# Routed-expert blocks: gathers for six more experts, weight halves on VectorE, evictions on ScalarE, and another order at the turn into the blocks

## What is computed

```python
scores = softmax(xt @ router_w + router_b) + router_bias      # 16 experts in 4 groups
# keep the 2 best groups, then the 2 best experts; vals = their scores; gate = vals scattered
def step(y, p):                                               # for each of the 16 experts
    h = silu(xt @ w1 + b1) * (xt @ w2 + b2)
    return y + ge[:, None] * (h @ w3 + b3)
z = (silu(xt @ sw1 + sb1) * (xt @ sw2 + sb2)) @ sw3 + sb3     # shared expert
```

## Time and profile before

| | |
|---|---|
| median of 3 runs | 608.7 us |
| profiled execution | 612.38 us, its span 610.6 us |
| mean granted TensorE clock | 0.992 |
| PE / DVE / ACT / POOL busy | 562.1 / 408.7 / 345.2 / 349.6 us |
| blocks, first matmul after the turn to last eviction | 110.6 to 184.6 us of the span |
| HBM read / written | 56.94 / 15.20 MB |

### The profile page before, as it was taken

How to read it: one execution, slowest core, us unless ns; L and a number is a source line. 1 busy time by engine, 2 the same in 40 slices (tenths; PEclk the granted TensorE clock), 3 DMA queues, 4 the chain that set the end, 5 groups by cost and what they waited for, 6 DMA issues and landing times.

```text
span 610.6 us, 11610 instructions
## 1 busy us (share of the span) xinstructions
PE 562.1 (92%) x3232; PEld 273.6 (45%) x3232; DVE 408.7 (67%) x1049; ACT 345.2 (57%) x858; POOL 349.6 (57%) x371
## 2 busy tenths in 40 slices
PE   2999998798969989999868999999999999999997
PEld 0445444576644444444313444444444344444453
DVE  6898756494535965555689999999999900001782
ACT  4575866543432276777666777877777723142131
POOL 5993375788956237989844544445444534477011
PEclk9999999899989999999989999999999999999999
DMA  9996289999968206989599999999999984342001
GB/s 338 413 383 244 53 214 199 253 383 408 396 236 308 89 10 181 204 202 214 114 224 175 180 169 182 180 178 183 180 179 182 174 172 167 105 152 87 2 1 69
DMA packets 211622, 118.78 MB, mean 195 GB/s; under 512 B 188017, under 2 KB 196337, under 8 KB 208642
## 3 DMA queue, kind: packets, MB, share of 16 engines
q1 hardware_dynamic: 209122, 108.58, 70.6%
q0 software_dynamic: 2288, 9.70, 4.3%
q10 hardware_dynamic: 176, 0.04, 0.0%
HBM read 56.94 MB, written 15.20 MB: 118 GB/s over the span
## 4 chain that ended last, share of the span: by engine, by line
PE 39%; POOL 19%; DVE 13%; issue 11%; SPq 8%; DMA 5%; ACT 4%; DVEq 0%; POOLq 0%; ACTq 0%
PE ps L358 12%; PE ps L360 11%; PE ps L359 11%; SPq L513 8%; POOL hlr L1317 5%; POOL wsp L1317 5%; POOL q_sb L1317 3%; PE ps L667 2%; PE ps L540 2%; POOL xs_dram L1358 1%; POOL pT L1317 1%; POOL q_sb L1334 1%; DMA stage<-in_moe,disp 1%; DMA wsp<-hlr 1%; POOL q_sb L1430 1%
## 5 line engine op out<-in xcount | busy, mean ns | idle before, releaser
L1188 ACT ACTIVATE f32r<-f32r,mneg 128x512 f32<-128x512 f32 x128 | 91.5, 715 | 29.0 <-DVE mneg L1895 29.0
L1317 POOL TENSOR_TENSOR wsp<-stage,wsp 128x512 f16<-128x512 f32 (+1 forms) x69 | 78.4, 1166 | 49.0 <-ACT wsp L1159 44.1
L1895 DVE CUSTOM_DVE_ANT_0 f32r<-ps,nmask 128x512 f32<-128x512 f32 x128 | 82.4, 680 | 1.5
L1453 POOL TENSOR_SCALAR hlr<-f32r,rinv 128x512 f16<-128x512 f32 x64 | 44.8, 708 | 48.9 <-DVE rinv L1900 45.1
L1453 POOL TENSOR_SCALAR stage<-f32r,rinv 128x512 f16<-128x512 f32 x64 | 43.6, 691 | 47.5 <-DVE rinv L1900 42.9
L1317 POOL TENSOR_TENSOR hlr<-f32r,hlr 128x512 f16<-128x512 f32 x36 | 41.3, 1158 | 44.5 <-ACT hlr L1269 33.6
L358 PE MATMUL ps<-q_sb 128*128 128x512 f16 x132 | 50.7, 384 | 14.6 <-POOL q_sb L1317 12.0
L358 PE MATMUL ps<-k_sb,q_sb 128*128 (+1 forms) x128 | 49.5, 387 | 11.7 <-DVE mneg L1895 8.9
L1905 DVE SCALAR_TENSOR_TENSOR hlr<-f32r,rinv,hlr 128x512 f16<-128x512 f32 x64 | 50.1, 818 | 1.3 <-POOL hlr L1453 1.3
L1905 DVE SCALAR_TENSOR_TENSOR stage<-f32r,rinv,stage 128x512 f16<-128x512 f32 x64 | 49.2, 807 | 2.3 <-POOL stage L1453 2.3
L360 PE MATMUL ps<-q_sb 128*128 128x512 f16 x132 | 50.5, 383 | 0.0
(11 more groups left out here) (365 smaller groups left out, 1427.1 us busy)
## 6 DMA issues: line engine op xcount, KB each, us to landing
stage<-in_wq SPq DMA_DIRECT2D x8, 1024.0 KB, 6.1
stage<-in_wo SPq DMA_DIRECT2D x8, 1024.0 KB, 4.8
q_sb<-in_moe SPq DMA_DIRECT2D x9, 768.0 KB, 9.1
xs_dram<-zeros SPq DMA_DIRECT2D x1, 5888.0 KB, 28.8
pT<-xs_dram SPq DMA_DIRECT2D x23, 256.0 KB, 7.5
r_dram<-f32r SPq DMA_DIRECT2D x23, 256.0 KB, 7.0
k_sb<-in_wkv SPq DMA_DIRECT2D x3, 1024.0 KB, 18.8
stage<-in_moe SPq DMA_DIRECT2D x4, 768.0 KB, 10.1
```

The lines of the kernel that those rows point to most:

```text
L1188: act.activation(f32r[:, j % 4, :], f32r[:, j % 4, :], ACT.Exp, bias=mneg[:, j % 4:j % 4 + 1], scale=-1.0, accum_out=psum_col[:, j % 4:j % ...
L1317: return pool.tensor_tensor(dst_lo, src, dst_hi, ALU.subtract)
L1453: pool.tensor_scalar(halves(j)[:, 0, :], f32r[:, j % 4, :], rinv[:, 0, j % 4:j % 4 + 1], PSCALE, ALU.mult, ALU.mult).then_inc(s_ph, 1)
L1895: dve.tensor_tensor_reduce(f32r[:, j % 4, :], ps[j % 4][:, :], nmask[:, qt, :], 0.125, BIG, ALU.add, ALU.min, mneg[:, j % 4:j % 4 + 1]).th ...
```

## The change

Weights of experts 8 to 12 and 14 are now gathered by POOL like those of the spill blocks. The row numbers that the gather uses lie beyond the table's end for an expert with no token, and for an unused spill block (the limit to expert 15 is gone); `bounds_check` with `oob_is_err=False` leaves such rows out. The lo halves from block 4 on are DVE's, the evictions ACT's; POOL keeps the lo halves of blocks 0 to 3, and those of 2 and 3 now stand in the key phase. At the turn ACT takes `silu(0)` ahead of the hi casts of key tiles 13 and 14, and DVE turns the rows of blocks 0 to 2 and gates block 0 ahead of normalising key tile 15.

```diff
+GATHERED = [8, 9, 10, 11, 12, 14] + list(range(E_ROUTED, NB))
 ...
@@ SP
-                if r == 13:
+                if r == 12:
                     load_slots(4)
 ...
-                    if BEFORE[m] == n - 2 and not E_ROUTED <= m < NB:
+                    if BEFORE[m] == n - 2 and m not in GATHERED:
                         load_expert(m)
@@ ACT
                         if ahead and r == r0 + tiles * iters - 1:
-                            ahead()
-                        if not first or j >= 1 + lag:
+                            ahead[0]()
+                            hi(r - 2, i, j - 2, first)
+                        if (not first or j >= 1 + lag) and not (ahead and r == r0 + tiles * iters - 2):
                             hi(r - 1 - lag, i if j >= 1 + lag else i - 1, (j - 1 - lag) % tiles, first)
 ...
+                if ahead:
+                    ahead[1]()
 ...
-                      {2: router_exponentials, 12: gates_split, 14: lambda: w12_hi(2)}, lambda: silu(0))
-            for n in range(1, NB):
+                      {2: router_exponentials, 12: gates_split, 14: lambda: w12_hi(2)},
+                      (lambda: silu(0), lambda: (w12_hi(3), silu(1))))
+            def evict(n):
+                act.wait_ge(s_dn, n + 1)
+                if n >= 3:
+                    act.wait_ge(s_rst[n % 3], 16 * (n // 3))
+                act.copy(f32r[:, n % 3, :], ps[n % 4][:, :]).then_inc(s_re, 1)
+            for n in range(2, NB):
                 silu(n)
                 w12_hi(n + 2)
+                evict(n - 2)
@@ POOL
+                if r == 14:
+                    w12_lo(2)
 ...
+                    if beside and j == 0:
+                        w12_lo(3)
 ...
+                i = GATHERED.index(n)
+                if i >= 4:
+                    pool.wait_ge(s_wi[i % 4], 16 * (i // 4))
+                rows = widx[:, n - E_ROUTED:n - E_ROUTED + 1] if n >= E_ROUTED else own_rows[:, n:n + 1]
+                pool.indirect_dma_start(landed_at(n, slice(0, EG)), None, moe, bass.IndirectOffsetOnAxis(ap=rows, axis=0),
+                                        bounds_check=E_ROUTED * P - 1, oob_is_err=False).then_inc(s_wi[i % 4], 16)
-            for n in range(NB):
-                w12_lo(n + 2)
-                for m in range(E_ROUTED, NB):
-                    if BEFORE[m] == n - 2:
-                        gather_expert(m)
+            for n in GATHERED:
+                gather_expert(n)
@@ DVE
+                link(dve.tensor_scalar(unowned, ps[6][:, NT * E_ROUTED:(NT + 1) * E_ROUTED], 0.0, 65536.0, ALU.is_equal, ALU.mult))
+                dve.scalar_tensor_tensor(out=own_rows, in0=first_slot, scalar=lane_less, in1=unowned, op0=ALU.add, op1=ALU.add)
 ...
-                link(dve.tensor_scalar(owner, owner, float(E_ROUTED - 1), None, ALU.min))
 ...
+            def first_rows():
+                slots_turned(0)
+                slots_turned(1)
+                gated(0)
+                slots_turned(2)
-                                            15: lambda: slots_turned(0)})
+                                            15: first_rows})
+            def w12_lo(n):
+                dve.wait_ge(s_w12h, n + 1)
+                for u in range(2):
+                    at = slice(u * KC * INTER, (u + 1) * KC * INTER)
+                    last = dve.tensor_tensor(split_at(n, 1, at), landed_at(n, at), split_at(n, 0, at), ALU.subtract)
+                last.then_inc(s_w12l, 1)
-            for n in range(NB):
-                if n + 1 < NB:
+            for n in range(1, NB):
+                if 2 < n + 1 < NB:
                     slots_turned(n + 1)
                 gated(n)
+                if n == 2:
+                    dve.wait_ge(s_w12l, 4)
+                if n >= 2:
+                    w12_lo(n + 2)
                 if n in (4, 6, 8):
                     (small_lows, owners_biases, pair_gates)[n // 2 - 2]()
-                if n >= 2:
-                    evict(n - 2)
```

More of the change, by code:

```diff
@@ L156, in xattn_ffn_kernel @@
         lane = disp[:, 56:57]
+        lane_less = disp[:, 57:58]
+        own_rows = sml[:, 0, :].bitcast(I32)
+        unowned = sml[:, 1, :]
         first_slot = disp[:, 60:60 + E_ROUTED]
@@ L378, in wait_landed @@
         def wait_landed(engine, n):
-            if E_ROUTED <= n < NB:
-                engine.wait_ge(s_wi[n % 4], 16 * ((n - E_ROUTED) // 4 + 1))
+            if n in GATHERED:
+                engine.wait_ge(s_wi[GATHERED.index(n) % 4], 16 * (GATHERED.index(n) // 4 + 1))
             else:
                 engine.wait_ge(s_we[LAND[n]], (32 if LAND[n] == 7 else 16) * (
-                    1 + sum(LAND[m] == LAND[n] and not E_ROUTED <= m < NB for m in range(n))))
+                    1 + sum(LAND[m] == LAND[n] and m not in GATHERED for m in range(n))))
         def wait_landing_free(engine, n):
@@ L1135, in _ @@
             rms_phase(0, 2, 8, 1.0 / HD, scs[:, 12:13], s_kT, True, True, None,
-                      {2: router_exponentials, 12: gates_split, 14: lambda: w12_hi(2)}, lambda: silu(0))
-            for n in range(1, NB):
+                      {2: router_exponentials, 12: gates_split, 14: lambda: w12_hi(2)},
[6 more added lines that the diff above has]
+            for n in range(2, NB):
                 silu(n)
                 w12_hi(n + 2)
+                evict(n - 2)
+            evict(NB - 2)
+            evict(NB - 1)
             def shared_silu(n, bank):
@@ L1546, in _ @@
             dve.tensor_copy(lane, ranked[:, E_ROUTED:E_ROUTED + 1])
+            dve.tensor_scalar(lane_less, ranked[:, E_ROUTED:E_ROUTED + 1], -1.0, None, ALU.add)
             dve.tensor_scalar(first_slot, ranked[:, 0:E_ROUTED], float(P), 1.0, ALU.mult, ALU.add)
@@ L1789, in slots_turned @@
                 dve.tensor_copy(words(turned(n)), ps[4 + n % 2][:, :].rearrange("p (l w) -> p l w", l=2)).then_inc(s_xTc, 1)
-            rms_phase(0, 2, 8, True, True, {3: scores_of_experts, 4: gates, 5: slot_numbers, 12: gates_turned, 13: owners,
-                                            15: lambda: slots_turned(0)})
-            def small_lows():
-                dve.wait_ge(s_mask, 16)
-                dve.tensor_scalar(nmask[:, :, :], nmask[:, :, :], -8.0, None, ALU.mult).then_inc(s_ol, 4)
-                dve.wait_ge(s_gh, 1)
-                dve.tensor_tensor(gatesT[1], gateT[0:E_ROUTED + 1, :], gatesT[0], ALU.subtract).then_inc(s_gl, 1)
             def bias(a, n):
@@ L1812, in gated, with small_lows @@
                                          in1=hidden[n % 3], op0=ALU.add, op1=ALU.mult).then_inc(s_hx, 1)
+            def first_rows():
[3 more added lines that the diff above has]
+                slots_turned(2)
+            rms_phase(0, 2, 8, True, True, {3: scores_of_experts, 4: gates, 5: slot_numbers, 12: gates_turned, 13: owners,
+                                            15: first_rows})
+            def small_lows():
+                dve.wait_ge(s_mask, 16)
+                dve.tensor_scalar(nmask[:, :, :], nmask[:, :, :], -8.0, None, ALU.mult).then_inc(s_ol, 4)
+                dve.wait_ge(s_gh, 1)
+                dve.tensor_tensor(gatesT[1], gateT[0:E_ROUTED + 1, :], gatesT[0], ALU.subtract).then_inc(s_gl, 1)
             def w3_lo(n):
```

10 lines of the change are left out of this document (removed).

## The result

The changed kernel took 607.28 us (median of 19 runs, 604.36 to 620.92), the kernel before, beside it, 610.24 us. The ratio is **0.9959**, with a 95% interval from 0.9943 to 0.9975: some 2.5 us faster (1.5 to 3.5), where 10.85 us were forecast. The time lies outside the forecast's range of 593 to 605 us, and the gain is 0.4%, where the forecast took 1% for the least that can be told from no change. The profiled execution took 607.73 us with a span of 606.0 (before 612.38 and 610.6); this one pair differs by 4.65 us, more than the interval of all runs, so its rows say where time is lost and not to a microsecond how much. Some executions of every kernel here take over 1% longer at a lower granted clock; the ratios leave them out, and two experiments (no late weights, the turn as before) were profiled in such an execution, so that only intervals inside it are read.

What follows compares the result with a forecast made beforehand. The prediction took DMA to bound the middle blocks, PE close behind. Gains and losses 10.55 - 0.5 - 1.0 + 1.2 + 0.6 = 10.85 us, so 608.7 - 10.85 = 597.8 us, range 593 to 605.

Steps and rivals of the forecast that it cites:

- What bounds the kernel: Blocks 4 to 22: DMA sets 3.29 us per block; dropping 4.7 MB leaves PE's 2.70 us, gaining 10.55 us.
- gathers eight blocks ahead: Blocks 7 to 16: gathers are issued eight blocks ahead, some 11 us to spare against their 7.4, helping hide the backlog.
- So most of the backlog is hidden. I take 1.0 us: Blocks 7 to 16: ten heavy loads make at most 5.9 us of DMA backlog, mostly hidden; loss 1.0 us.
- The first rival: Middle blocks: DMA still sets the pace, ten blocks at 3.29 us, 5.9 us lost, 602.7 us in all; chance 0.18.
- allowance of 8.2 us for stores: Evictions on ACT, waiting for the store three blocks before: a store landing of up to about 8.2 us costs nothing.
- The turn. Gain 1.2 us: Turn into the blocks: block 5's rows issued about 115.2, landing 3.9 us later, silu(4) about 120.4; gain 1.2 us.
- The end. Gain 0.6 us: From silu(22) to the last eviction: 2.5 us at full clock instead of 3.1; gain 0.6 us.
- The lo halves: Moved from POOL to DVE: DVE's block takes 2.32 us, below PE's 2.70; loss 0.5 us beside DVE's small sums.
- that rival: Lo halves on DVE are slow, 1.64 us each as while POOL subtracted; about 625 us; chance 0.02.
- Rows moved all the same: Gathers: rows out of range are moved anyway or as slowly, 3.29 us per block stays, 606.9 us; chance 0.07.
- Gathers that starve: POOL from block 9: gather issues progress only while DVE idles, 21 us lost, about 619 us; chance 0.05.
- HBM reads lower by 4.7 MB: Sign that the forecast is right: HBM reads at 52.2 MB; 56.9 MB would speak for the second rival.

Runs made afterwards that it cites:

- no late weights: Changed kernel with the gathers' bound leaving out all rows for block 14 and blocks 16 to 22, so none of their weights load: 600.87 us, ratio 0.9818.
- the turn as before: Changed kernel with the turn into the blocks put back as in the kernel before; gathers, lo halves and evictions stay changed: 605.32 us, ratio 0.9915.
- the rows early: Changed kernel with SP loading the rows of blocks 5 to 7 between the last key transposes instead of behind them: 602.88 us, ratio 0.9864.
- both orders and the fourth buffer: Changed kernel with rows of blocks 5 to 7 loaded early, blocks with weights spread among empty experts, and a fourth result buffer: 597.58 us, ratio 0.9796.
- the blocks spread: Changed kernel with blocks reordered so that experts without tokens stand among those with gathered weights, same bytes: 601.48 us, ratio 0.9865.
- the fourth buffer alone: Changed kernel with only a fourth result buffer, so evictions wait for the store four blocks before: 604.43, 605.22, 617.07 and 618.34 us, no interval.
- the roles as before: Changed kernel with all blocks' lo halves back on POOL and evictions back on VectorE; new gathers and turn stay: 610.09 us, ratio 1.0001.
- the transfers as before: Changed kernel with experts 8 to 12 and 14 loaded plainly and the unused spill block gathering expert 15's weights again: 610.79 us, ratio 1.0016.

## Why the prediction was wrong

**What bounds the kernel: right in part.** Transfers held blocks 9 to 22, and rows that are left out are really not moved: all queues together moved 4.7 MB less. But the 5.14 us won between `silu(4)` and `silu(22)` aren't a faster middle. Blocks 9 to 19 took 0.80 us more than before, blocks 4 to 9 0.65 more, and blocks 19 to 22 6.59 less. The prediction had booked block 22's wait as a wait for bytes alone. Its "gathers eight blocks ahead" doesn't hold for that block: its landing place is that of block 16, and POOL issued it at 168.40, 3.4 us before the cast wanted it (4.10 us of wait, ending at 175.85), so that POOL's own work, which the change took away, was part of the wait.

**"So most of the backlog is hidden. I take 1.0 us" failed, by about 4.** This is the step that decided. With the 0.5 us for VectorE the blocks were to lose 1.5 us of 10.55, and they lost 5.41 (54.01 - 48.6). The first rival happened almost as written: ten blocks, 9 to 19, at 3.29 us, 5.9 us above PE's pace, with ScalarE waiting for stores. The reason lies in the step ahead: a mean pace of 3.29 us over 18 blocks was read as every block's pace because 1.31 MB at 398 GB/s gives the same number. It was a chance: 2.70 us up to block 9, and 3.51 behind it. The loads that went had been moved beside blocks that ran at PE's pace, and the ten heavy ones stayed in a row where the waits had been. The argument for hiding them set an allowance of 8.2 us for stores against a median of 7.0, and a median says nothing of the stretch in which all queues are full: the stores issued from 138 to 149 us took 9.4 to 13.2 us. The earlier trace rows already had the hint: PE busy 28.4 of 29.4 us up to 140, and 31.27 of 35.8 from there on. Spreading the heavy blocks gave the missing time back without a byte saved. And a store later than the allowance was dearer than before: with the evictions on ScalarE, ahead of `silu`, it held PE, for an estimated 2 to 3 us of the 5.9 (the table above).

**"The turn. Gain 1.2 us" failed by 2.2 in the profiled execution; why rows landed late there and not elsewhere stays open.** The issue was foreseen within 0.1 us (115.33 against 115.2). The landing was taken as 3.9 us and was 5.0, and no price was set for what PE does behind a wait: the first turning and `up` ran in part on the lower clock, 2.35 us from turning to `silu(4)` instead of 1.32, another 1.0. In the four other executions with this turn PE had rows 3.0 to 3.7 us after the issue and `silu(4)` came at 119.61 to 120.80, around the forecast's 120.4; in three of them PE paid for the lower clock all the same. There the forecast's time came out, in part by luck: the landing was shorter than 3.9 us and the clock's price, left out, was 1.0. SP's order, which the change left alone, was worth more than either. A sooner start of blocks 0 to 3 (`silu(0)` by 2.4 us) mostly lengthened PE's wait for the rows of block 5, from nothing to 2.5 to 4.5 us, and loading those rows between the transposes shortened block 3 to 4 from 6.05 to 8.44 us to 3.59 to 4.73.

**"The end. Gain 0.6 us" failed, by about 1.** The evictions kept 0.18 of it. The cast that waits for the shared expert's weights stands ahead of all three on ScalarE, which the text didn't list, although the evictions' move put them behind it. PE's last `down` began at 178.06 and took about 0.9 us, so without the cast the last eviction could have begun near 179.0 (an estimate); it began near 179.7. From their end to the first gather it took 3.63 us against 3.07, so that in all 0.38 us were lost there.

The three errors, 3.9 + 2.2 + 1.0, are the 7.1 us between 10.85 and 3.73 in this pair of executions. Only the first recurs in another (53.28 us with the rows early).

**The lo halves: right.** A pair took 1.28 us on VectorE and none waited for it in the heavy blocks:

```profile
112.97 2.21 DVE L1855 TENSOR_TENSOR wsp<-q_sb,wsp 128x512 f16<-128x512 f32 x2
...
115.96 1.28 DVE L1855 TENSOR_TENSOR wsp<-v_sb,wsp 128x512 f16<-128x512 f32 x2
```

The 2.21 is the only slow one, and POOL was subtracting beside it (112.86 to 114.03); that rival needed POOL's operation and there were none left. The Trainium skill ("SBUF — State Buffer", SBUF: two separate sides) has an operation of VectorE with two SBUF inputs share the lock only with a GpSimd operation that reads SBUF; by 2.21 against 1.28 us the trace agrees. Blocks 7 to 8 and 9 to 10, with VectorE's small sums near them, took 3.04 and 2.92 us against PE's 2.70, together 0.6 over, near the 0.5 allowed; no wait in the trace names VectorE, so that it was the cause isn't shown. What the text didn't count is that the move of the lo halves also frees POOL, which otherwise needs 3.47 us for a block with a gather and sends the last gathers late.

**The rivals.** The first came true, as said. Rows moved all the same: no. Gathers that starve: no, but not for nothing; see below. "HBM reads lower by 4.7 MB" was a wrong sign: that row of the page still says 56.94 MB, while the queues moved 114.07 instead of 118.78 MB. Why it didn't follow was not tried.

## What to carry to other kernels

A mean pace over a loop is no block's pace: list the intervals first, and count a saved byte only where it would have been moved while something waited. When heavy transfers follow one another, put the light blocks between them before saving more, and compare the free time of a wait with the landings of the fullest stretch, never with a median. Do not put a wait for a store ahead of work that feeds PE. A consumer that starts sooner gains little if the load it waits for is issued behind unchanged work, and a wait of PE can cost its clock as well. And profile a second execution before a difference of 2 us is explained.

## What the runs showed of the hardware

An indirect DMA whose rows are all out of range isn't free of packets. The queue of these gathers, in the kernel before and after (packets, MB, share of 16 engines):

```profile
q0 software_dynamic: 2288, 9.70, 4.3%
```

```profile
q0 software_dynamic: 3152, 9.70, 4.5%
```

The change makes six more gathers, 13 for 7, and six of the 13 are empty. The packets rose by 864, or 144 for each more, while the MB stayed those of seven full ones: an empty gather has a full one's packets (the seven full ones of the kernel before have 1,008 in the blocks) and next to no bytes. The six landed after 2.5 to 6.1 us, the seven full ones after 7.8 to 9.6; these are the issues from 125 to 127 us, a load of rows and an empty gather:

```profile
pT<-xs_dram SPq DMA_DIRECT2D x1, 256.0 KB, 2.5
q_sb<-in_moe,sml POOLq DMA_INDIRECT x1, 2.5
```

A gather's issue on POOL took 0.957 us before, 0.98 to 1.44 after, with VectorE's lo halves beside most, and 1.01 to 1.05 when those were back on POOL:

```profile
133.45 1.44 POOL L1439 DMA_INDIRECT q_sb<-in_moe,sml  x1 [4.03 <-PE ps L671]
...
147.50 1.14 POOL L1439 DMA_INDIRECT q_sb<-in_moe,disp  x1 [1.55 <-PE ps L671]
```

The Trainium skill ("SBUF — State Buffer", SBUF: two separate sides) has a DMA from POOL held up while VectorE runs a two-port operation, by a factor of about five in its example. The sign agrees; here it was 1.5 at most, with VectorE busy 9.59 of 10 us from 126 to 136, and it delayed nothing. One issue in the kernel with both orders and the fourth buffer took 1.99 us. Which operations of VectorE lengthen an issue no run here shows.

The two kinds of stretch also show how far a landing depends on what else is in the queues: with 222 to 241 GB/s (issues from 116 to 134 us) 256 KB landed after 2.0 to 5.8 us, with 357 to 416 GB/s (issues from 136 to 155 us) after 6.2 to 14.9.

PE's clock did not follow the length of its wait at the turn. Behind waits of 4.54, 3.30, 3.20 and 2.54 us for rows (the change, the blocks spread, the fourth buffer alone, the roles as before) the granted clock fell to the lower level (0.50 in the first turning's microsecond); behind one of 3.17 us (the transfers as before) it stayed at 1.00, and the first turning took 0.62 us.
